# Value transposes moved from TensorE to VectorE and a way through memory, in a gated-delta-rule attention and MLP kernel

## The reference, cut to what matters

```python
mixed = jnp.einsum('bsh,ch->bsc', x, W_qkv)                # projections q, k, v
conv = sum(xp[:, k:k+Ss, :] * conv_w[:, k] for k in range(4))
mixed = silu(conv)                                         # then split in q, k, v
q, k = l2n(q), l2n(k)
A = -(einsum(k_beta, kc) * decay) * strict                 # per chunk
Tm = inverse(I - A)
u = Tm @ v_beta
# scan over chunks, state S (128x128 per value head):
attn = (q @ k.T) * decay
v_new = u - kcd @ S
out = (q*exp(g)) @ S + attn @ v_new
S = S*exp(g_last) + (k*exp(g_last-g)).T @ v_new
...
core * rsqrt(mean(core^2)) * norm_w * silu(z)  ->  W_out
```

## Time and profile before

| | before |
|---|---|
| median of 3 runs | 4351.33 us |
| time of the profiled execution | 4346.94 us |
| its span | 4345.1 us |
| granted TensorE clock, mean | 0.988 |
| TensorE matmul busy | 4173.4 us (96%) |
| VectorE busy | 3617.4 us (83%) |
| ScalarE busy | 2591.5 us (60%) |
| GpSimd busy | 3023.5 us (70%) |
| DMA engines busy | 31.6% (mean 79 GB/s) |

### The profile page before, as it was taken

One profiled execution on the slowest core, in us unless ns is written; L12 is line 12 of the kernel. 1 busy time (PEld: TensorE's weight loads), 2 busy tenths in 40 slices (PEclk: granted clock), 3 DMA queues, 4 the chain that ended last, 5 costly groups with the idle time before them and its releaser, 6 DMA issues. The chain is left out here.

```text
span 4345.1 us, 91653 instructions
## 1 busy us (share of the span) xinstructions
PE 4173.4 (96%) x29748; PEld 3125.8 (72%) x29748; DVE 3617.4 (83%) x7996; ACT 2591.5 (60%) x5684; POOL 3023.5 (70%) x8984
## 2 busy tenths in 40 slices
PE   5799999999999999999999999999999999998798
PEld 2577777777777777777777777777777777776465
DVE  6788898888888888888888888888888888886554
ACT  3566666666666666666666666666666666665221
POOL 1777777777777777777777777777777777775221
PEclk8899999999999999999999999999999999999999
DMA  5333333333233333333233323333333323331100
GB/s 153 74 77 80 92 73 77 79 86 89 64 94 81 89 68 82 79 99 87 66 92 83 89 65 82 82 99 82 70 90 85 89 65 82 82 79 39 69 15 25
DMA packets 877310, 342.30 MB, mean 79 GB/s; under 512 B 741920, under 2 KB 826400, under 8 KB 867616
## 3 DMA queue, kind: packets, MB, share of 16 engines
q1 hardware_dynamic: 876832, 336.43, 31.6%
HBM read 255.44 MB, written 80.86 MB: 77 GB/s over the span
## 5 line engine op out<-in xcount | busy, mean ns | idle before, releaser
L954 DVE SCALAR_TENSOR_TENSOR CV<-pp,CW,CV 128x1023 f32<-128x1023 f32 (+2 forms) x768 | 979.2, 1275 | 19.4 <-ACT CV L1541 12.6
L409 PE MATMUL pp<-A,W 128*128 128x512 f32 x2048 | 973.7, 599 | 12.2 <-DVE CV L954 9.5
L1981 POOL TENSOR_TENSOR UL<-UL,TM 128x126 f32<-128x126 f32 (+22 forms) x1984 | 734.7, 370 | 155.5
L1978 POOL TENSOR_TENSOR TM<-UL,XL 128x126 f32<-128x126 f32 (+22 forms) x1984 | 699.9, 353 | 145.5 <-DMA XL<-xb 8.8
L1097 DVE SCALAR_TENSOR_TENSOR St<-St,TAB,kv 128x128 f32<-128x128 f32 x1024 | 309.8, 344 | 347.8 <-PE kv L546 342.8
L1641 ACT ACTIVATE VS<-qa,EB 128x128 f32<-128x128 f32 x1024 | 320.3, 366 | 465.8 <-PE qa L536 465.8
L409 PEld LDWEIGHTS pp<-A,W 128*128 128x128 f32 x2048 | 368.7, 193 | 281.5 <-issue 266.9
L590 PE MATMUL emit<-Wo,NTr 128*128 128x256 f32 x2048 | 497.0, 385 | 3.1 <-ACT NTr L1674 3.1
L569 PE MATMUL emit<-Wz,A 128*128 128x256 f32 x2048 | 495.7, 385 | 0.8 <-DVE A L1148 0.8
L590 PEld LDWEIGHTS emit<-Wo,NTr 128*128 128x128 f32 x2048 | 373.5, 190 | 93.5 <-issue 29.7
L1630 ACT ACTIVATE QE<-qa,TAB 128x128 f32<-128x128 f32 x1024 | 317.6, 362 | 179.5 <-PE qa L526 177.8
(11 more groups left out here) (231 smaller groups left out, 8796.4 us busy)
## 6 DMA issues: line engine op xcount, KB each, us to landing
GB<-gcd SPq DMA_DIRECT2D x64, 1024.0 KB, 5.6
W<-wqkv SPq DMA_DIRECT2D x256, 128.0 KB, 3.7
kb<-TB SPq DMA_DIRECT2D x256, 128.0 KB, 3.5
XL<-xb SPq DMA_DIRECT2D x128, 256.0 KB, 3.9
K<-kb SPq DMA_DIRECT2D x64, 512.0 KB, 5.1
UL<-c_u SPq DMA_DIRECT2D x64, 256.0 KB, 2.9
xb<-X SPq DMA_DIRECT2D x512, 32.0 KB, 1.6
Wz<-wz SPq DMA_DIRECT2D x64, 256.0 KB, 4.8
```

The source lines that it names most:

```text
L409: ins = t.matmul(bk.pp[:, 512 * h:512 * h + 512], m.W[:, c, k, :], m.xnT[:, w // KH % 2, c, 512 * h:512 * h + 512], start=c == 0, stop=c == 1)
L954: v.scalar_tensor_tensor(m.CV[:, t, d:S], bk.pp[:, 0:S - d], m.CW[:, w % KH, t, 3 - d:4 - d], m.CV[:, t, d:S], ALU.mult, ALU.add).then_inc ...
L1978: gp.tensor_tensor(m.TM[:, 0:a, 0:b], m.UL[:, 0:a, k:k + 1].to_broadcast([128, a, b]), m.XL[:, k, k + 1:32].unsqueeze(1).to_broadcast([128 ...
L1981: gp.tensor_tensor(m.UL[:, 0:a, k + 1:32], m.UL[:, 0:a, k + 1:32], m.TM[:, 0:a, 0:b], ALU.subtract).then_inc(s["sub"], 1)
```

## The change: values transposed on VectorE, moved through memory

`tpv` and `vev` are gone. In their place a unit has, for each of its two value heads `r`:

- `vsl(w, r)` on ScalarE: Silu over `CV[:, 2+r]` in place, 128x1024.
- `vtr(w, r)` on VectorE: a transpose of 32x32 blocks from `CV[:, 2+r]` into `CV[:, r]`, 128x1024.
- `vto(w, r)` on SyncE: four DMAs from `CV[:, r]` to memory, 128-byte pieces; `vti(w, r)`: one DMA back into `V`.

`CV[:, 0]` and `CV[:, 1]` are where `cv0` of the next unit's q and k writes, so `cv0(w, 0)` and `cv0(w, 1)` now also wait until `vto` of the unit before has landed. `vsc` waits for both `vti`.

```diff
+    def vto(w, r):
+        sp.wait_ge(s["vtr"], 2 * w + r + 1)
+        sp.wait_ge(s["dvi%d" % r], 16 * w)
+        for i in range(4):
+            q.dma_start(dr.vb[r, :, :, :, i, :].rearrange("a p c d -> p c a d"),
+                        m.CV[32 * i:32 * i + 32, r].rearrange("p (c a d) -> p c a d", a=4, d=32)).then_inc(s["dvo%d" % r], 16)
+    def vti(w, r):
+        sp.wait_ge(s["dvo%d" % r], 64 * (w + 1))
+        sp.wait_ge(s["R"], CH * (w - 1))
+        q.dma_start(m.V[w % 2][:, :, r, :], dr.vb[r].rearrange("a p c g d -> (a p) c (g d)")).then_inc(s["dvi%d" % r], 16)
-    def tpv(w, r, h):
-        pe.wait_ge(s["cvk"], 3 * tile_count(w, 2 + r) + 3)
-        for c in range(4):
-            ins = t.transpose(bk.strip[:, c * 128:(c + 1) * 128], m.CV[:, 2 + r, (4 * h + c) * 128:(4 * h + c + 1) * 128],
-                              g.ident)
+    def vtr(w, r):
+        dv.wait_ge(s["vsl"], 2 * w + r + 1)
+        dv.wait_ge(s["kp"], w + 1)
+        v.transpose(m.CV[:, r, :], m.CV[:, 2 + r, :]).then_inc(s["vtr"], 1)
         if t == 0:
             ac.wait_ge(s["kp"], w)
+            ac.wait_ge(s["dvo0"], 64 * w)
         elif t == 1:
             ac.wait_ge(s["kt"], w)
             ac.wait_ge(s["kp"], w)
+            ac.wait_ge(s["dvo1"], 64 * w)
-    def vev(w, r, h):
-        a.activation(m.V[w % 2][:, 4 * h:4 * h + 4, r, :], by(bk.strip[:], 4), ACT.Silu).then_inc(s["strip"], 1)
+    def vsl(w, r):
+        a.activation(m.CV[:, 2 + r, :], m.CV[:, 2 + r, :], ACT.Silu).then_inc(s["vsl"], 1)
...
         for u in range(1, NU - 2):
+            vtr(u, 0)
             state(u - 1, 0)
...
+            vtr(u, 1)
             state(u - 1, 2)
```

More of the change, by code:

```diff
@@ L325, in loop @@
         ldg(2)
+        vto(0, 0)
+        vti(0, 0)
+        vto(0, 1)
+        vti(0, 1)
         uo(0)
@@ L344, in loop @@
         ldt(1)
+        vto(1, 0)
+        vti(1, 0)
+        vto(1, 1)
+        vti(1, 1)
         uo(1)
@@ L361, in loop @@
         for u in range(1, NU - 2):
+            index(u + 2)
+            decoded(u + 1)
+            sto(u - 2)
+            vto(u + 1, 0)
             ldt(u + 1)
-            index(u + 2)
-            sto(u - 2)
-            decoded(u + 1)
             ldg(u + 3)
-            ldo(u + 1)
+            vti(u + 1, 0)
+            vto(u + 1, 1)
+            vti(u + 1, 1)
             uo(u + 1)
@@ L370, in loop @@
             nl(u + 1)
+            kto(u + 2)
+            kti(u + 2)
+            ldo(u + 1)
             ui(u + 2)
+            ldw(u + 3, 2)
             xo(u + 2, 0)
-            ldw(u + 3, 2)
-            kto(u + 2)
+            ldz(u + 1)
             xo(u + 2, 1)
-            xl(u + 2)
             ldw(u + 3, 3)
-            kti(u + 2)
             ldw(u + 3, 0)
             ldx(u + 4)
-            ldz(u + 1)
+            xl(u + 2)
+        vto(NU - 1, 0)
+        vti(NU - 1, 0)
+        vto(NU - 1, 1)
+        vti(NU - 1, 1)
         ldt(NU - 1)
@@ L676, in loop @@
         m2(0)
-        tpv(1, 0, 0)
         m3(0)
@@ L1246, in loop @@
         cvk(0, 3, 3)
+        vtr(0, 0)
+        vtr(0, 1)
         lm(0, 2)
@@ L1361, in loop @@
         core(NU - 3, 0)
+        vtr(NU - 2, 0)
         r_(NU - 3, 1)
@@ L1372, in loop @@
         core(NU - 3, 2)
+        vtr(NU - 2, 1)
         seed(NU - 3, 0)
@@ L1435, in loop @@
         core(NU - 2, 0)
+        vtr(NU - 1, 0)
         r_(NU - 2, 1)
@@ L1444, in loop @@
         core(NU - 2, 2)
+        vtr(NU - 1, 1)
         seed(NU - 2, 0)
@@ L1733, in loop @@
         cv0(0, 3)
-        vev(0, 0, 0)
+        vsl(0, 0)
+        vsl(0, 1)
         cv0(1, 0)
-        vev(0, 0, 1)
-        vev(0, 1, 0)
         qt(1)
@@ L1740, in loop @@
         kt(1)
-        vev(0, 1, 1)
         qsq(1)
@@ L1754, in loop @@
         y2(0, 0)
-        vev(1, 0, 0)
+        vsl(1, 0)
         vs(0, 0)
@@ L1758, in loop @@
         vne(0, 0)
-        vev(1, 0, 1)
         qe(0, 1)
@@ L1821, in loop @@
             sq(u, 0)
-            vev(u + 1, 0, 1)
+        vsl(NU - 2, 1)
         qe(NU - 3, 2)
@@ L1831, in loop @@
         cv0(NU - 1, 1)
-        vev(NU - 2, 1, 0)
         qe(NU - 3, 4)
@@ L1835, in loop @@
         sq(NU - 3, 1)
-        vev(NU - 2, 1, 1)
         vs(NU - 3, 4)
@@ L1869, in loop @@
         vne(NU - 2, 0)
-        vev(NU - 1, 0, 0)
+        vsl(NU - 1, 0)
         sz(NU - 3, 3)
@@ L1877, in loop @@
         sq(NU - 2, 0)
-        vev(NU - 1, 0, 1)
+        vsl(NU - 1, 1)
         qe(NU - 2, 2)
@@ L1885, in loop @@
         vne(NU - 2, 3)
-        vev(NU - 1, 1, 0)
         qe(NU - 2, 4)
@@ L1889, in loop @@
         sq(NU - 2, 1)
-        vev(NU - 1, 1, 1)
         vs(NU - 2, 4)
```

164 lines of the change are left out of this document (75 added, 89 removed), and 2 rows, old and new, of the table SEMS.

## The result

The changed kernel takes 4555.68 us in the median of 4 runs (4553.24 to 4557.53), the kernel before 4353.07. The ratio is 1.0466, with an interval of 1.0453 to 1.0479. The forecast was 4370 us and its range ended at 4420. The direction was right, the size was not: 24 us were forecast and 203 came.

What follows compares the result with a forecast made beforehand. Bound by the larger of two limits per turn: two halves (61.1 plus 0.2 for the DMA, 61.3 us) and the GpSimd loop (61.5). 0.4 us over 61.09, times 61, is 24 us: 4347 + 24 = 4371, said as 4370; range 4305 to 4420.

Steps and rivals of the forecast that it cites:

- the loop through GpSimd: `seed` on VectorE, GpSimd's `on` and `sub` chain, `nrm`, `vt`, next `seed`: forecast 61.5 us a turn on average.
- the two halves: Turn split at `state` 3: first half TensorE-bound, 19.29 us; second with VectorE full, 41.8; together 61.1 us.
- TensorE loses 1.76 us a turn: Four `tpv` a turn at 0.44 us each leave TensorE; the saving was forecast to lie off the path.
- The full half with `vtr`: `state` 3 to next `state` 0, VectorE full, first `vtr` added at its end: 41.8 us forecast, 41.4 to 42.6.
- The second `vtr`: Stands in the first half of the turn, where VectorE has idle time: forecast to cost nothing.
- The way to memory: `cv0` waits for `vtr` data to land in memory, delaying `nt` and `op`: 0.2 us a turn, 0 to 0.9.
- From `vt` to `seed` ... 18.4: Last piece of the GpSimd loop: 17.60 us of before, plus a `red` and two X rows, less an `oacc`.
- the term "4.88": Piece of the GpSimd loop from `nrm` through the six steps behind it to `vt`: 4.88 us, as before.
- VectorE's transposes hold up GpSimd: Rival: GpSimd stands still during each `vtr`, adding 2.5 us to the `sub` chain each turn; 4524 us, chance 0.03.
- Outside the loop: First turns with more transposes and late DMAs, last two losing `tpv` slots: forecast 0, plus or minus 5 us.
- The way to memory comes late: Rival: data land 6.7 us into the turn, delaying `cv0` and `op`; 62.3 us a turn, 4421 us, chance 0.12.
- TensorE as the bound: Rival: VectorE's list closes its gaps, GpSimd keeps up, turn falls by up to 1.76 us, to 4240; chance 0.24.

Runs made afterwards that it cites:

- the old order: The change's way for the values through memory, with the loop lists of all five queues in the order of the kernel before: 4418.65 us, ratio 1.0153.
- the two runs with most of the hold gone: Changed kernel with both `gm` moved together behind `on(u, 2)`: 4489.62 us; changed kernel with each `gm` cut into four instructions at its place: 4489.09 us.

## Why the prediction was wrong

**The bound.** Right. The busy share of TensorE meant nothing, and the loop through GpSimd and the two halves are the two limits. In the new order the loop decides: `nrm` waits for `ty`, the turn is 63.6 with `vtr` and 64.3 without it, and when the last piece of the loop lost 1.77 us and its first gained 0.55, the turn fell by 1.29. In the old order the halves decide.

**TensorE loses 1.76 us a turn, worth nothing.** Right. `ks` now waits 48.5 us for `St` in all against 18.7 before, 0.5 a turn where 1 was forecast, and TensorE is busy 59.90 us of the turn, where some 59 was forecast. One detail was read wrongly: the `tpv` at 2000.39 does start inside the first half. It is the one that was set at nothing, and the half stayed at 19.28 us (1460.43 to 1479.71).

**The full half with `vtr`, 41.8 (41.4 to 42.6).** In the old order, where this half decides, the measured 42.39 lies in the range and 0.6 above the value taken. I had counted on gaps that would close; only the 0.48 at the end of the half gave way. In the changed kernel the half lasts 44.31 us with VectorE busy 42.95, the holds below included. The second `vtr` at nothing was right.

**The way to memory, 0.2 (0 to 0.9).** Right in size. In a typical turn after the change the data land 5.7 us behind `state` 0:

```profile
1466.20 1.11 ACT L1565 ACTIVATE CV<-pp,CW 128x1024 f32<-128x1024 f32 x1 [0.93 <-DMA vb<-CV]
```

It delays `nt` behind it (the earlier trace rows for before), and `op` on TensorE waited 16.7 us in all for `NTr` after the change, where it had waited 3.1:

```profile
L613 PE MATMUL emit<-Wo,NTr 128*128 128x256 f32 x2048 | 499.5, 387 | 17.0 <-ACT NTr L1695 16.7
...
L539 PE MATMUL kv<-St,QK 128*128 128x256 f32 x1024 | 345.4, 419 | 49.6 <-DVE St L1111 48.5
```

That is 0.2 us a turn on average. The second row is the wait of `ks` named above. Not foreseen was the turn in which a load of 1 MB is issued before it, 12.8 us in the old order.

**The loop through GpSimd: this is the step that failed.** "From `vt` to `seed` ... 18.4" was the sum of the durations of before, and it is right for instructions that are not held: 18.67 and 18.70 in the two runs with most of the hold gone. The list of after puts both `gm`, 2.35 us each, where VectorE comes to `ty` and `wv`; they are held 1.10 and 1.06 us, and 20.44 is measured. Taking most of the hold away in two ways gives 66 and 67 us, of which 61 and 65 are in the 60 turns. It is not all of the 2.04 us a turn (122 us in 60 turns), because `seed` to the first `sub` then takes 0.5 us longer, with GpSimd waiting that long for issue; the turn stays at 62.3, not 61.8.

A third hold was overlooked. `krb`'s `SS<-SS` stands in the term "4.88" from `nrm` to `vt`, and the new place of `vsc` beside it costs 0.30 us there. The term still came out at 4.96, in part since 0.14 us of waiting for `strip` had gone. All runs in the new order have this hold, so what it costs the turn was not tested.

The clue lay in the kernel before. Its `ty` takes 157 ns at least and 419 at most, its `wv` 0.35 typically and 381 ns in the mean: the same work with a varying duration pointed at something that it waits for. I did have the rival "VectorE's transposes hold up GpSimd" at 0.03, and it was right to be low: `sub` keeps its pace beside `vtr` (the chain takes 30.6 us in the median turn before and after). But I asked only whether the *added* instruction holds another, and not whether the *moved* ones are held. The Trainium skill, "SBUF — State Buffer", section "SBUF: two separate sides", states the rule for both directions: of a GpSimd instruction and a VectorE one of the kinds named in the prediction, whichever starts first keeps the shared port pair to its end. The trace agrees, with 1.26 us for an instruction of 0.16. The same section of the Trainium skill counts VectorE instructions with two SBUF inputs among them, against a GpSimd one that reads SBUF, which is what the run without `TENSOR_SCALAR` showed at 1.26 us; had I read that clause again, I would not have expected a gain from that form.

**Outside the loop, 0 plus or minus 5 us.** It was 47 us. +25 in the last two turns, of which some 13 is the load of TAB that stands behind waiting transfers on SyncE, and +22 in the first. The order does this without the way through memory too: 111.3 us in the first turn and 128.0 in the last two, against 100.1 and 120.3. What in the order lengthens the first turn was not found; it is 111 to 123 us in the kernels with the new order and varies with small edits.

**The rivals.** None was what happened. "The way to memory comes late" decided a single turn only, in the old order. TensorE as the bound, 0.24, found no support. The chance of "slower", 0.51, was right, and the range was too narrow on its upper side: it held only unknown waits of the added instructions, and nothing for five rewritten lists.

So of the 203 us 61 to 65 went with the hold in the two runs, 47 lie outside the loop, and the other 92 to 96 are the rest of the new order in the loop. With most of the hold gone a typical turn is 62.3 against 61.09: 73 us in 60 turns, mostly 1.07 us more between `vt` and `seed` than in the old order (18.67 against 17.60), 0.39 of it the hold that remains on `wv`, and the issue wait before `sub`. The remainder, some 20 us, is in single turns that are longer, the change of batch among them. The way through memory has no part in the sum, since its cost lies off the path.

## What to carry to other kernels

When a change comes with rewritten instruction lists, run the two apart: here the order was the whole loss, and the algorithmic step cost nothing on top of it, but 66 us in the order that suits the kernel. A sum of durations from the old trace holds only for instructions that meet the same neighbours on other engines; for each small VectorE instruction between SBUF and SBUF on the critical loop, ask which long GpSimd instruction will run beside it, and cut that one into pieces or move it. A list that waits in order, as SyncE's does, must have the transfers that are wanted first in front of the ones that must wait.

## What the runs showed of the hardware

- A GpSimd `TENSOR_TENSOR` of 128x1024 (2.35 us) holds a VectorE instruction of 128x4 from SBUF to SBUF until it ends: 1.26 us for 0.16. It holds `TENSOR_SCALAR` and `SCALAR_TENSOR_TENSOR` with two operands in SBUF alike. A `V<-V,RK` of the same size (1.89 us) holds a `TENSOR_SCALAR` of 128x16 to 0.49 us from 0.19.
- Beside the same `gm`, `TENSOR_SCALAR` from PSUM (`Y<-mr`, 0.70 us) is not held: its mean is 697 ns before, where none of its 64 starts falls in a `gm`, and after, where 61 do. Nor is `STREAM_TRANSPOSE` from SBUF to SBUF: the 63 `vt` steps that start beside a 1.89 us `V<-V,RK` take 0.70 us.
- Cut into four GpSimd instructions in a row, `gm` holds `ty` to the end of the piece that runs, 0.32 us in place of 1.26. The cut costs 0.43 us per `gm` (2.78 against 2.35).
- TensorE's granted clock was 0.66 in the 10 us behind a stretch in which TensorE waited for work that a late transfer had delayed, part of them at 1.2 GHz. With the transfer moved it was 1.00 there.
